# First weights of all eight experts kept in SBUF, with a VectorE copy by register into the four-deep ring, in a mixture-of-experts kernel

## The reference

```python
def _token_moe(h, gate_W, gate_b, exp_W1, exp_b1, exp_W2, exp_b2):
    flat = h.reshape(-1, D)                       # 4096 tokens x 128
    logits = flat @ gate_W + gate_b
    top_v, top_i = jax.lax.top_k(logits, 2)       # 2 of 8 experts
    w = jax.nn.softmax(top_v, axis=-1)
    w_full = jnp.zeros((N, 8)).at[jnp.arange(N)[:, None], top_i].add(w)
    for e in range(8):
        mid = jax.nn.gelu(flat @ exp_W1[e] + exp_b1[e], approximate=False)   # 128 -> 512
        out = out + w_full[:, e:e + 1] * (mid @ exp_W2[e] + exp_b2[e])       # 512 -> 128
```

## Time and profile before

| | us |
| --- | --- |
| median of 3 runs | 775.77 |
| lowest, highest | 774.07, 776.71 |
| the profiled execution's own time | 775.02 |
| its span, from first to last instruction | 773.2 |
| its block stage: first row transpose to last | 568.8 to 743.7 |
| PE busy in the span | 579.9 (75%) |
| DVE busy in the span | 426.1 (55%) |

### The profile page before, as it was taken

How to read it: one execution, slowest core, us unless ns; L and a number is a source line. 1 busy time by engine, 2 the same in 40 slices (tenths; PEclk the granted TensorE clock), 3 DMA queues, 4 the chain that set the end, 5 groups by cost and what they waited for, 6 DMA issues and landing times.

```text
span 773.2 us, 15557 instructions
## 1 busy us (share of the span) xinstructions
PE 579.9 (75%) x4384; PEld 461.9 (60%) x4385; DVE 426.1 (55%) x1285; ACT 230.8 (30%) x559; POOL 321.8 (42%) x327
## 2 busy tenths in 40 slices
PE   0463897988877978978879778795249999998960
PEld 0362576666655657656566566564148887787860
DVE  4424456686767676576685774673513433333435
ACT  0101313414313403313322331331024444444430
POOL 5302341451464563463562562463714334334340
PEclk9755758887979878879787898797559999999995
DMA  5996260250430250170000000000135555555639
GB/s 131 176 205 108 62 78 2 68 71 1 92 54 15 77 76 8 31 120 14 14 0 7 22 0 9 14 8 28 41 106 158 149 158 153 157 158 147 166 95 322
DMA packets 90461, 63.85 MB, mean 83 GB/s; under 512 B 16302, under 2 KB 77105, under 8 KB 90420
## 3 DMA queue, kind: packets, MB, share of 16 engines
q1 hardware_dynamic: 86100, 54.86, 33.0%
q0 software_dynamic: 4320, 8.47, 3.1%
HBM read 35.18 MB, written 28.58 MB: 82 GB/s over the span
## 4 chain that ended last, share of the span: by engine, by line
PE 55%; DVE 15%; issue 11%; ACT 4%; SPq 4%; POOL 4%; DMA 3%; DVEq 1%; another core or an unknown queue 1%; ACTq 0%; POOLq 0%
PE bank L678 9%; PE bank L667 7%; PE bank L497 6%; PE bank L522 5%; PE bank L380 4%; PE bank L451 4%; PE bank L437 3%; PE bank L385 2%; PE bank L480 2%; DVE places L1102 2%; PE bank L509 2%; PE bank L429 2%; PE bank L481 2%; POOL sorted_rows L983 2%; PE bank L502 2%
## 5 line engine op out<-in xcount | busy, mean ns | idle before, releaser
L1046 POOL DMA_INDIRECT result_rows<-back,rows x71 | 69.4, 978 | 117.6 <-DVE back L1466 109.8
L845 ACT ACTIVATE mid<-bank,b 128x128 f32<-128x128 f32 x284 | 81.2, 369 | 92.3 <-PE bank L667 80.5
L522 PEld LDWEIGHTS bank<-vbd,pT 128*128 128x128 f32 x512 | 74.6, 216 | 44.4 <-issue 24.2
L963 POOL TENSOR_TENSOR km<-kb,head 128x512 f32<-128x512 f32 x56 | 59.5, 1069 | 80.2 <-ACT kb L752 49.1
L678 PE MATMUL bank<-w,mid 128*128 x568 | 83.8, 292 | 11.0 <-ACT mid L845 9.2
L678 PEld LDWEIGHTS bank<-w,mid 128*128 128x128 f32 x568 | 71.2, 194 | 24.2 <-issue 23.0
L667 PE MATMUL bank<-hT,w 128*128 128x128 f32 x568 | 83.0, 291 | 3.1 <-DMA w<-in_L_ffn_exp_W_dram 1.6
L522 PE MATMUL bank<-vbd,pT 128*128 128x36 f32 x512 | 74.2, 295 | 13.9 <-ACT pT L765 13.1
L914 POOL TENSOR_TENSOR rs<-ve,minus_half 128x12 f32<-128x12 f32 (+2 forms) x24 | 39.8, 1660 | 97.4 <-DVE ve L1149 48.5
L667 PEld LDWEIGHTS bank<-hT,w 128*128 128x128 f32 x568 | 71.1, 197 | 5.9 <-issue 4.4
L497 PE MATMUL bank<-km,qbd 128*128 128x512 f32 x128 | 73.3, 658 | 0.0
(11 more groups left out here) (187 smaller groups left out, 1004.1 us busy)
## 6 DMA issues: line engine op xcount, KB each, us to landing
w<-in_L_ffn_exp_W_dram SPq DMA_DIRECT2D x79, 256.0 KB, 3.4
sorted_rows<-blank SPq DMA_DIRECT2D x64, 260.0 KB, 7.6
rows<-sorted_rows SPq DMA_DIRECT2D x71, 65.0 KB
places<-result_rows SPq DMA_DIRECT2D x16, 256.0 KB, 5.5
places<-in_ctx_dram SPq DMA_DIRECT2D x8, 256.0 KB, 2.9
places<-in_x_dram SPq DMA_DIRECT2D x8, 256.0 KB, 3.8
out_dram<-acc SPq DMA_DIRECT2D x8, 256.0 KB, 5.9
result_rows<-back,rows POOLq DMA_INDIRECT x71
```

The lines of the kernel that those rows point to most:

```text
L522: last = pe.matmul(pv_bank[:, hp * W:hp * W + W].rearrange("p (b c) -> p b c", b=BPT), pT[:, j, :], vbd[u][:, t, :, hp, :], start=True, st ...
L845: A(mid[s][:, c, :], hidden[2 * s + c // 2][:, c % 2 * P:c % 2 * P + P], ACT.Gelu, bias=b1[:, bass.ds(expert, 1), c]).then_inc(mid_ok, 1)
L963: G.tensor_tensor(km[n % 2][:, :, :], kb[u][:, n % 2, t * S:t * S + S].unsqueeze(1).broadcast_to([P, HG, S]), head8[:, :].unsqueeze(2).bro ...
L1046: G.indirect_dma_start(out=result_dram, out_offset=bass.IndirectOffsetOnAxis(ap=rows[s][:, D:D + 1].bitcast(U32), axis=0), in_=back[s % 4] ...
```

## The change

The first weights of all eight experts are loaded once into `w1_all`, a view over two slabs of `places` that the attention stage has finished with; SyncE issues these eight DMAs of 256 KB after the last group's projection (`vf_ps`), ahead of its wait for the scatters. In the block stage SyncE loads the rows alone. `turn` on VectorE gets a second half: it reads the block's expert into a register, waits until TensorE is through with block i - 4, and copies 128x512 fp32 out of `w1_all` into the ring of four. `middle` waits for this copy (`w1_ok`) and not for a DMA.

```diff
+        w1_all = places[:, 1:3, :, :, :].rearrange("p a u t d -> p (a u) (t d)")
...
+                sp.wait_ge(vf_ps, GROUPS)
+                for e in range(E):
+                    sp.dma_start(w1_all[:, e, :], a["L0_ffn_exp_W1"][e]).then_inc(w1_loaded, 16)
...
                 def load_block(i, s):
-                    turn, turn4 = (i - s) // RING, (i - s % 4) // 4
-                    expert = sp.value_load(expert_of[0:1, bass.ds(i, 1)], min_val=0, max_val=E - 1)
+                    turn = (i - s) // RING
                     place_of = sp.value_load(row_of[0:1, bass.ds(i, 1)], min_val=0, max_val=SPARE + (GROUPS - 1) * P)
...
                     sp.dma_start(rows[s][:, :], sorted_dram[bass.ds(place_of, P), :]).then_inc(row_loaded[s], 16)
-                    if not (isinstance(i, int) and i < 4):
-                        sp.wait_ge(mid_ps, 2 * i - 6)
-                    sp.dma_start(w1[s % 4][:, :], a["L0_ffn_exp_W1"][bass.ds(expert, 1)].rearrange("o p h -> (o p) h"))\
-                      .then_inc(w1_loaded[s % 4], 16)
...
                 def middle(i, s):
                     pe.wait_ge(rT_ok, i + 1)
-                    pe.wait_ge(w1_loaded[s % 4], ((i - s % 4) // 4 + 1) * 16)
+                    pe.wait_ge(w1_ok, i + 1)
...
                     V.tensor_scalar(hT[s % 2][:, :], turned[s % 2][:, 0:P], cols[:, G2], cols[:, B2], ALU.mult, ALU.add)\
                         .then_inc(rT_ok, 1)
+                    expert = dve.value_load(expert_of[0:1, bass.ds(i, 1)], min_val=0, max_val=E - 1)
+                    if not (isinstance(i, int) and i < 4):
+                        dve.wait_ge(mid_ps, 2 * i - 6)
+                    V.tensor_copy(w1[s % 4][:, :], w1_all[:, bass.ds(expert, 1), :].rearrange("p o h -> p (o h)"))\
+                        .then_inc(w1_ok, 1)
...
                 dve.wait_ge(moe_loaded, (2 * E + 2) * 16)
+                dve.wait_ge(w1_loaded, E * 16)
```

More of the change, by code:

```diff
@@ L219, in xattn_attention_moe @@
         scattered = sems("scattered0 scattered1")
-        w1_loaded = sems("w1_loaded0 w1_loaded1 w1_loaded2 w1_loaded3")
+        w1_loaded, w1_ok = sems("w1_loaded w1_ok")
         row_loaded = sems(" ".join(f"row_loaded{i}" for i in range(RING)))
```

## The result

The changed kernel takes 811.32 us (median of 4 runs, 811.22 to 813.74) against 775.05 for the kernel before in the same runs (774.07 to 776.71): a ratio of 1.0473, 95% interval 1.0445 to 1.0501. It is slower by 36 us, where +22 was forecast; 811 lies within the range of 790 to 821, but above the 806 at which the forecast's own bounds end, in the band of 806 to 821 that was given to a slow copy or load chain, with a chance of 0.12. The profiled execution has a span of 809.4 us.

What follows compares the result with a forecast made beforehand. The prediction took PE's own pace, 2.48 us per block, as the bound. A closed chain of 2.82 us over 67 intervals added 22.6 us, less 0.5 at the start: 798 us, range 790 to 821.

Steps and rivals of the forecast that it cites:

- a slow copy or load chain: Rival: VectorE's copy takes 0.69 us, or its load chain is slower; 816 us, band 806 to 821, chance 0.12.
- The ring: Block stage: transpose, turn, register load, copy, `middle`, next transpose form a closed chain of 2.82 us per block against 2.48.
- The cover of 1.11 us: Time on PE from a block's row transpose to its `middle`, into which VectorE's added work must fit; 0.28 us free.
- Turn to copy: On VectorE, from turn's start to the copy's start, register load included: 0.88 us, bounds 0.67 and 0.91.
- Copy's end to `middle`: From the end of VectorE's copy to PE's start of `middle`: 0.11 us, between 0.05 and 0.2.
- The copy: VectorE's 128x512 copy of the weight, per block: 0.42 us, bounds 0.42 and 0.69.
- The step that failed: Block stage before the change: PE's own pace of 2.48 us sets it; the removed weight transfer causes only one 1.62 us stall.
- Hidden after all: Rival: VectorE reads the register while waiting for the transpose, the interval stays 2.48 us; 773.7 us, chance 0.05.
- GpSimd and the copy: Rival: VectorE's copy must wait for the end of GpSimd's indirect DMA, 3.25 us per block; 827 us, chance 0.13.
- The register load: VectorE's load ahead of the copy: 312 ns by the trace; by the skill's floor of about 600 ns, 817 us.
- The clock: Rival: PE's clock falls in half of the blocks, 0.57 us more in each; 817 us, chance 0.04.
- The weights' early loads: Eight transfers, 2 MB, before the block stage: 13.5 us within over 65 us, hidden, costing nothing.

Runs made afterwards that it cites:

- ahead: The changed kernel with the copy for block i + 3 put behind the turn of block i + 2: 763.29 us, 0.988 of the kernel before.
- beside: The kernel before plus early weight loads, and VectorE's register load and copy into a scratch tile that PE does not wait for: 775.72 us, ratio 1.004.
- fixed: The changed kernel without the register load ahead of the copy, which takes expert block mod 8: 763.49 us, 0.988 of the kernel before.
- sp_light: The kernel before without SyncE's register load of the expert; its 256 KB DMA takes expert block mod 8: 754.30 us, ratio 0.972.
- reuse_flat: The changed kernel with the copy one block earlier, the expert kept in a register until weighing, and VectorE's loop written out: 751.85 us, 0.969 of the kernel before.
- oneport: The changed kernel with the copy written as a multiplication by a column of ones: 812.92 us, 1.052 of the kernel before.

## Why the prediction was right in kind and short in size

- **The ring** was right in each of its links, and right in that it decides: 3.05 us per block, shown by ahead (link taken away, 2.37) and by beside (work kept, wait taken away, 2.55). The cover of 1.11 us was the right thing to measure against.
- **Its terms** were mis-sized, 2.82 where 3.05 was measured (3.09 inside the loop, 2.8 to 2.9 in the blocks before and behind it). Transpose to turn 0.42 and `middle` to transpose 0.99 came out to the hundredth. Turn to copy was 0.96 instead of 0.88, outside the upper bound of 0.91: I had named one more register instruction than the row of 0.91 has and still took less than the row. Copy's end to `middle` was 0.24 instead of 0.11, outside 0.2. The copy was 0.48 on average instead of 0.42. These are 0.08 + 0.13 + 0.06 = 0.27 on the ring's steps, as in the loop; over all 67 intervals it is 0.23, and 67 x 0.23 = 15 us is what the forecast missed. The forecast's own bounds ended at 806. That 811 lies in the range is owed to the band for a slow copy or load chain, priced at 816 on a copy of 0.69 throughout, and there was no such copy: three smaller misses came to about as much. To that extent the range held by luck. Both queue steps are longer inside the loops, where waits and addresses are worked out in registers. In the blocks behind the loop, written out with constants, they are 777.66 - 776.88 = 0.78 and 0.10:

```profile
776.88 0.41 DVE L1455 TENSOR_SCALAR hT<-bank,cols 128x128 f32<-128x128 f32 x1 [0.57 <-PE bank L659]
...
777.66 0.65 DVE L1460 COPY w<-places 128x512 f32 x1 [0.37 <-issue]
```

  In fixed, the step from turn to copy is 0.33 inside the loop and outside. So on VectorE the loop's part hangs on the register load and the addresses, not on the wait that both have; which of them was not taken apart.

- **The step that failed** is in the first part: that the stage goes at PE's own pace, and that of the removed work only a stall of 1.62 us had cost anything. SyncE's queue set the pace. I read the waits of PE and took the queue without waits for one without a role; a queue that never waits over 170 us is the one that is full. The row that told it in PE's terms, 21.6 us of "issue" ahead of `output` from 600.8 to 745, was passed over for the 9.2 us of gelu. So was a sum from the earlier trace rows: the block shown there takes 0.99 + 1.11 = 2.10 us from transpose to transpose and not 2.48. That 2.10 is PE's own pace (the median interval of sp_light and of reuse_flat is 2.13); the other 0.38 is what the prediction put down to gelu and PE's register load. It did no harm to the forecast only because the new ring is longer than SyncE's round and covers what its relief brings.
- **Hidden after all**: not what happened, and its price was wrong for the same reason. Where the copy is out of the way the kernel is at 0.988 and not, as 773.7 would be, at 0.997 of the kernel before.
- **GpSimd and the copy**: true in part. The copy waits for a part of the indirect DMA, up to 0.29 us, in 21 of 71 blocks, 4.0 us in all, not the 29 of the rival that held it excluded for the whole length. The Trainium skill, SBUF — State Buffer, section Who interferes with whom, says that copies and the one-input multiplication can run in the mode that takes the ports shared with GpSimd, and that the two hold them in turn. That agrees with the change (21 of 71 copies stretched) and with oneport (15 of 71). That a GpSimd instruction holds them for its whole length is not so for the indirect DMA: a copy that began 0.46 us into one took 0.43, and so did those of ahead that began 0.1 us into one.
- **The register load** is 0.31 us in the changed kernel too. The floor of about 600 ns that the Trainium skill, DMA: Bandwidth & Descriptors, section Latency and other measured facts, gives is not seen. With the register work and the address behind it the load costs 0.63 us of the ring (fixed), and that is the number to reckon with.
- **The clock** stayed full from 575 us to the end of the stage, at a PE share of 29.94 / 40 = 0.75. (Its rival was priced with 18 records per block. A block has 8 + 1 + 8 = 17, so at 3.20 us for 17 it would have cost 0.38 us in half of the blocks, 13 us, and not 19.) **The weights' early loads** cost nothing that shows; the stage even began 2 us sooner, where 0.5 was forecast.

## What to carry to other kernels

Before putting an instruction on an engine with idle time, ask whether it comes between two steps that wait for each other: then its latency counts, with the register work ahead of it, and idle time is no cover; the same copy one block ahead no longer held PE up (there VectorE's own round then set the pace). A queue that issues DMAs can be the bound while nothing waits for it by name: look for the queue that never waits, and for data that is issued just ahead of its use. Taking work off such a queue pays only if the engine that takes it over doesn't close a longer ring.

## What was not expected of the hardware

- A register load on SyncE's queue in a loop with two DMAs per block was worth 22 us over 71 blocks (sp_light, with the address worked out from it), with 256 KB per block of traffic unchanged.
- The same step of VectorE's queue, register load and copy, costs 0.96 us in a loop and 0.78 in code written out with constants, and PE's answer to the copy 0.24 and 0.10.
- A fast-form copy of 128x512 (0.427 us) that begins 0.51 to 0.69 us into an indirect DMA of GpSimd (0.98 us) ends 0.25 us after it, and so takes 0.53 to 0.71 us; one that begins earlier, or later than 0.8 us, takes 0.05 us more at most. A two-input form of the same size took 0.691 to 0.694 in all 71, five of which began in that part.
- Two chips differ by 2.4% on one kernel (757.5 and 776.0 us), so that single times of different sets can't be compared.
